# Layer 1 of a two-layer graph network: sums laid out by node, target one-hot made on ScalarE, and node blocks finished and stored inside the edge loop

## The reference, cut to what matters

```
h = relu(layernorm(x))                       # per node
z = h @ W;  el, er = <z, attn_l>, <z, attn_r>  # 8 heads of 16
e = leaky_relu(el[src] + er[dst], 0.2)
a = exp(e - segment_max(e, dst)[dst])
x = x + segment_sum(z[src] * a, dst) / segment_sum(a, dst) + bias     # layer 1

h = relu(layernorm(x))                       # per node, needs layer 1 complete
s, v = h @ W_up_s, h @ W_up_v                # the table that layer 2 gathers
w = mlp(edge_attr_8)                         # 8 -> 64 -> 64 -> 128
m = products of (s, v)[src], edge_attr_4, w  # 256 values an edge
x = x + W_out(segment_sum(m, dst) / 10)                               # layer 2
```

## Time and profile before

| | us |
|---|---|
| median of three runs | 4102.19 |
| the profiled execution | 4099.62 |
| its span | 4097.8 |
| PE busy | 3675.0 (90%) |
| PE weight load busy | 2848.9 (70%) |
| DVE busy | 1874.9 (46%) |
| ACT busy | 568.4 (14%) |
| POOL busy | 3007.4 (73%) |

### The profile page before, as it was taken

How to read it: one execution, slowest core, us unless ns; L and a number is a source line. 1 busy time by engine, 2 the same in 40 slices (tenths; PEclk the granted TensorE clock), 3 DMA queues, 4 the chain that set the end, 5 groups by cost and what they waited for, 6 DMA issues and landing times.

```text
span 4097.8 us, 68625 instructions
## 1 busy us (share of the span) xinstructions
PE 3675.0 (90%) x18070; PEld 2848.9 (70%) x18071; DVE 1874.9 (46%) x4776; ACT 568.4 (14%) x1289; POOL 3007.4 (73%) x3153
## 2 busy tenths in 40 slices
PE   2899999999999999999969889888898988899888
PEld 2677777777777777777757677666676776677666
DVE  7333333333333333333355555555555555555555
ACT  2111111111111111111131111111111111111111
POOL 3777777777777777777747777777777777777776
PEclk9555555555555555555568889898988988898998
DMA  3222222222222222222222222222222222222221
GB/s 85 56 57 57 57 57 57 57 57 57 57 57 57 57 57 57 57 57 57 57 53 59 59 60 59 60 59 60 59 59 60 59 60 59 60 60 59 59 60 51
DMA packets 259082, 239.78 MB, mean 59 GB/s; under 512 B 179890, under 2 KB 205596, under 8 KB 259068
## 3 DMA queue, kind: packets, MB, share of 16 engines
q0 software_dynamic: 100352, 212.14, 19.1%
...
q10 hardware_dynamic: 144, 0.80, 0.1%
...
...
## 4 chain that ended last, share of the span: by engine, by line
POOL 68%; issue 24%; DVE 3%; DMA 2%; PE 1%; POOLq 1%; DVEq 1%; ACT 0%; SPq 0%; ACTq 0%
POOL rows L406 68%; DMA rows<-up_tab,idx 1%; PE pair L942 1%; DVE share L895 1%; DVE dst_rel L570 0%; DVE share L885 0%; POOLq L220 0%; POOLq L434 0%; POOLq L221 0%; DVE share L770 0%; DVE share L627 0%; DVE share L898 0%; DVEq L226 0%; DMA win_dram<-share 0%; PE pair L937 0%
## 5 line engine op out<-in xcount | busy, mean ns | idle before, releaser
L406 POOL DMA_INDIRECT rows<-z_tab,idx x1568 | 1487.8, 949 | 544.2 <-issue 544.2
L406 POOL DMA_INDIRECT rows<-up_tab,idx x1568 | 1479.4, 944 | 510.8 <-issue 505.6
L1012 PE MATMUL pair<-share 128*128 128x48 f32 x3136 | 1008.0, 421 | 0.0
L1012 PEld LDWEIGHTS pair<-share 128*128 128x128 f32 x3136 | 802.9, 317 | 191.7 <-issue 184.4
L1093 PEld LDWEIGHTS pair<-share 128*128 128x128 f32 x3136 | 585.8, 219 | 454.8 <-DVE share L898 285.9
L1095 PE MATMUL pair<-share 128*128 128x144 f32 x3136 | 846.6, 359 | 0.0
L1093 PE MATMUL pair<-share 128*128 128x48 f32 x3136 | 576.9, 269 | 156.5 <-DVE share L898 154.3
L895 DVE TENSOR_TENSOR share<-rows,pair 128x384 f32<-128x384 f32 x784 | 396.9, 548 | 437.7 <-DMA rows<-up_tab,idx 409.1
L1095 PEld LDWEIGHTS pair<-share 128*128 128x128 f32 x3136 | 552.6, 220 | 0.0
L1014 PE MATMUL pair<-share 128*8 128x48 f32 x3136 | 516.2, 265 | 0.0
L806 DVE TENSOR_TENSOR share<-rows,pair 128x64 f32<-128x64 f32 x196 | 43.4, 221 | 855.0 <-DMA rows<-z_tab,idx 763.0
...
## 6 DMA issues: line engine op xcount, KB each, us to landing
rows<-z_tab,idx POOLq DMA_INDIRECT x1568
rows<-up_tab,idx POOLq DMA_INDIRECT x1568
...
ef_sb<-in_edge_f SPq DMA_DIRECT2D x198, 32.0 KB
...
y_sb<-in_edge_y SPq DMA_DIRECT2D x198, 16.0 KB
...
```

The lines of the kernel that those rows point to most:

```text
L406: pool.indirect_dma_start(out=rows[:, s, t, 0:width], out_offset=None, in_=table, in_offset=bass.IndirectOffsetOnAxis(ap=indices[:, t:t + ...
L1012: t.matmul(bank[2 + h][:, 0:WIN], msg[:, h, i, :], hot[:, s, i, :], start=(i == 0), stop=(i == T - 1), skip_group_check=True)
```

## The change

- Sums of layer 1 are formed node-major: the one-hot (now edge by 128 lanes) is the stationary operand and the messages the moving one, with exp(score) itself as a 17th column of each head, so the denominators come out of the same product. A sum goes into one of 98 half-block slots (`slot_i`), 136 wide. Rows of z_tab have 144 numbers, with ones in the 17th columns.
- The turned one-hot is no longer turned by TensorE. SyncE broadcasts the group's 1024 targets to all partitions (`load_targets`, from `dst_tab`, a float copy of the targets written to DRAM at the start), and ScalarE makes relu(1 - 2 (dst - node)^2) of it in two passes (`turned_hot`).
- The scores take three operations. `er` stays in SBUF (`er_slots`) and TensorE reads it from there by slot.
- A complete block is divided, normalized, turned, projected with `w_up`, and stored into up_tab in the loop (`finish_block`, `norm_block`, `map_up`, `store_up`). The middle stage for all blocks is gone; what is left there is the last blocks.
- Accumulators of layer 2 are cleared by VectorE and ScalarE behind the loop. All of `src` is loaded once; ScalarE copies a group's indices out of it (`set_idx`), in both layers, in place of a DMA a group.
- The set-up gets the operations that the slots need (`set_windows`), the float copy of the targets, and other memsets.

```diff
+RW = PER_HEAD + 1
+MW = HEADS * RW
+ZW = MW + HEADS
+LW = ZW + HEADS
...
+            def load_targets(s, group):
+                sp.dma_start(dst_bc[:, s % 2, :], dst_tab[bass.ds(group * GE, GE)].partition_broadcast(P)).then_inc(s_l1["in"][s % 2], 16)
+
+            def store_up(b):
+                sp.wait_ge(s_mid["row"], b + 1)
+                sp.dma_start(up_tab[bass.ds(b * P, P), :],
+                             sums_even[:, bass.ds(b, 1), 0, 0:HIDDEN].rearrange("p a f -> p (a f)"))\
+                  .then_inc(s_mid["stored"], 16)
...
+                    for s in range(U):
+                        hold(sp, s_l1["turned"], m + (s + AHEAD + 1))
+                        load_targets(s, q * U + (s + AHEAD))
+                        if s == 2:
+                            blocks(sp, q + 1, store_up)
+
+            last_blocks(sp, store_up)
...
-            pool.memset(er_win[:], 0.0).then_inc(zeroed, 1)
-            pool.memset(acc_b[:], 0.0).then_inc(zeroed, 1)
-            pool.memset(acc_a[:], 0.0).then_inc(zeroed, 1)
...
+            pool.memset(slot_i[:], 0).then_inc(zeroed, 1)
+            pool.memset(sums_all, 0.0).then_inc(zeroed, 1)
+            pool.memset(er_slots, 0.0).then_inc(zeroed, 1)
+            pool.memset(minus_id, 0.0).then_inc(zeroed, 1)
...
-                if s_l is s_l2:
-                    pool.wait_ge(s_mid["agg_staged"], NB)
-                    pool.memset(den_acc, 0.0).then_inc(zeroed, 1)
-                    pool.memset(max_acc, 0.0).then_inc(zeroed, 1)
-                    pool.memset(acc_a[:], 0.0).then_inc(zeroed, 1)
-                    table_stored(s_mid)
...
+            gather_edges(s_l1, s_l1["msg"], z_tab, ZW, passes1, 0)
+            pool.wait_ge(s_mid["stored"], 16 * NB)
+            gather_edges(s_l2, s_l2["prod"], up_tab, HIDDEN, passes, passes1 * GI)
...
+            def set_idx(s, group):
+                nc.scalar.activation(idx[:, s, :], idx_all[:, bass.ds(group, 1), :].rearrange("p a t -> p (a t)"),
+                                     ACT.Copy).then_inc(idx_set, 1)
+
+            def turned_hot(s, group, arrived):
+
+                act.wait_ge(s_l1["in"][s % 2], arrived)
+                to = hotT[:, s % 2, :]
+                nc.scalar.activation(to, dst_bc[:, s % 2, :], ACT.Square, bias=minus_id[:, bass.ds(group, 1)])\
+                    .then_inc(s_l1["square"], 1)
+                act.wait_ge(s_l1["square"], squares(group))
+                nc.scalar.activation(to, to, ACT.Relu, bias=ones[:, 0:1], scale=-2.0).then_inc(s_l1["turned"], 1)
+
+            def norm_block(b):
+
+                act.wait_ge(s_mid["mean"], b + 1)
+                nc.scalar.activation(hc_sb, x_sb[:, bass.ds(b, 1), :].rearrange("p a f -> p (a f)"), ACT.Relu,
+                                     bias=nmr1).then_inc(s_mid["centred"], 1)
+                nc.scalar.activation(std1, mv1[:, 1:2], ACT.Sqrt, bias=flags[:, 7:8]).then_inc(s_mid["norm"], 1)
+                act.wait_ge(s_mid["turned"], b + 1)
+                nc.scalar.activation(hcT_sb, bank[0][:, 0:P], ACT.Copy).then_inc(s_mid["turned_sb"], 1)
...
+            last_blocks(act, norm_block)
+            act.wait_ge(s_mid["stored"], 16 * NB)
+            nc.scalar.activation(acc[:, COLS:AUX], flags[:, 7:8].broadcast_to([P, AUX - COLS]), ACT.Copy, scale=0.0)\
+                .then_inc(G["cleared"], 1)
...
+
+                def floor_of(out, at, scale, shift):
+                    own.after(v.tensor_scalar(out, at, scale, shift, ALU.mult, ALU.add))
+                    own.after(v.tensor_scalar(out, out, ROUND, -ROUND, ALU.add, ALU.add))
+
+                floor_of(slot_f[:, :], win_f[:, :], 1.0 / HALF, -(HALF - 1) / (2.0 * HALF))
+                own.after(v.tensor_copy(slot_i[0:1, 1:NG + 1], slot_f[0:1, :]))
+                floor_of(odd_f[:, :], slot_f[:, :], 0.5, -0.25)
+                own.after(v.scalar_tensor_tensor(out=odd_f[:, :], in0=odd_f[:, :], scalar=-2.0, in1=slot_f[:, :],
+                                                 op0=ALU.mult, op1=ALU.add))
+                own.after(v.tensor_scalar(slot_f[:, :], slot_f[:, :], float(HALF), None, ALU.mult))
+
+                own.after(v.scalar_tensor_tensor(out=minus_id[:, 0:NG], in0=odd_f[:, :], scalar=col2[:, 1:2],
+                                                 in1=slot_f[:, :], op0=ALU.mult, op1=ALU.subtract))
+                own.after(v.tensor_scalar(minus_id[:, 0:NG], minus_id[:, 0:NG], col2[:, 0:1], None, ALU.subtract))
+                own.after(v.scalar_tensor_tensor(out=slot_f[:, :], in0=odd_f[:, :], scalar=-float(HALF),
+                                                 in1=slot_f[:, :], op0=ALU.mult, op1=ALU.add))
+                own.after(v.tensor_scalar(odd_f[:, :], odd_f[:, :], float(P), None, ALU.mult))
+                cols = dst_col[:, 0:NG, :]
+                own.after(v.tensor_tensor(cols, dst_rel[:, :, :], bc(slot_f[:, :], 2, T), ALU.subtract))
+                turn_back = tab_sb[:, 0:BU + 4, :].rearrange("p a f -> p (a f)")[:, 0:NG * T]\
+                    .rearrange("p (g t) -> p g t", t=T)
+                own.after(v.scalar_tensor_tensor(out=turn_back, in0=cols, scalar=float(P), in1=bc(odd_f[:, :], 2, T),
+                                                 op0=ALU.is_ge, op1=ALU.mult))
+                own.after(v.tensor_tensor(cols, cols, turn_back, ALU.subtract))
...
             def one_hot(s, group):
-
                 v.tensor_tensor(hot[:, s, :, :],
-                                bc(dst_rel[:, bass.ds(group, 1), :].rearrange("p a t -> p (a t)"), 2, WIN),
-                                bc(iota_l1, 1, T), ALU.is_equal).then_inc(s_l1["hot"], 1)
+                                bc(dst_col[:, bass.ds(group, 1), :].rearrange("p a t -> p (a t)"), 2, P),
+                                bc(iota_l1, 1, T), ALU.is_equal)
...
+            def finish_block(b):
+
+                own_block.base, own_block.n = b * 9, 0
+                even = sums_even[:, bass.ds(b, 1), 0, :].rearrange("p a f -> p (a f)")
+                odd = sums_even[:, bass.ds(b, 1), 1, :].rearrange("p a f -> p (a f)")
+                before = sums_odd[:, bass.ds(b, 1), 0, :].rearrange("p a f -> p (a f)")
+                own_block.mark(v.tensor_tensor(even[HALF:P], even[HALF:P], odd[HALF:P], ALU.add))
+                own_block.after(v.tensor_tensor(even[0:HALF], even[0:HALF], before[0:HALF], ALU.add), hold)
+                cells = even.rearrange("p (h f) -> p h f", f=RW)
+                own_block.after(v.tensor_scalar(rden, cells[:, :, PER_HEAD], TINY, None, ALU.max), hold)
                 own_block.after(v.reciprocal(rden, rden))
...
+                        own_l1.mark(v.tensor_tensor(e_sb[:, h, :, 0, :], el_e, er_e[:, :, 0, :], ALU.add))
+                        own_l1.after(v.scalar_tensor_tensor(out=e_sb[:, h, :, 1, :], in0=el_e, scalar=NEG_SLOPE,
+                                                            in1=er_e[:, :, 1, :], op0=ALU.mult, op1=ALU.add))
+                        v.tensor_tensor(e2_sb[:, h, :, :], e_sb[:, h, :, 0, :], e_sb[:, h, :, 1, :], ALU.max)\
+                            .then_inc(s_l1["score"], 1)
...
+            last_blocks(dve, finish_block)
+            v.memset(acc[:, 0:COLS], 0.0)
+            own.after(v.memset(acc[:, AUX:4 * COLS], 0.0))
...
+            def targets_er(s, group, count):
+
+                h = s % 2
+                at = pe.value_load(slot_i[0:1, bass.ds(group + 1, 1)], min_val=0, max_val=SLOTS1 - 1)
+                pe.wait_ge(s_l1["turned"], count + (AHEAD + 1))
+                for i in range(T):
+                    mm = t.matmul(bank[6 + h][:, i * 16:i * 16 + 16], hotT[:, h, i * P:(i + 1) * P],
+                                  er_flat[:, bass.ds(at, 1), :].rearrange("p a f -> p (a f)"), start=True, stop=True)
+                mm.then_inc(s_l1["er"], 1)
+
+            def map_up(b):
+
+                pe.wait_ge(s_mid["centred"], b + 1)
+                t.transpose(bank[0][:, 0:P], hc_sb, ident[:, :]).then_inc(s_mid["turned"], 1)
+                pe.wait_ge(s_mid["turned_sb"], b + 1)
+                pe.wait_ge(s_mid["row"], b)
+                t.matmul(bank[1][:, 0:P], hcT_sb, w_up[:, :], start=True, stop=True).then_inc(s_mid["lin"], 1)
...
+                                pe.wait_ge(s_l1["msg"], n * (2 * U) + (2 * U + 2 * s + i // HT + 1))
+                            if i == 0:
+                                pe.wait_ge(s_l1["added"], n * U + (s + 1))
+                            mm = t.matmul(bank[2 + h][:, 0:MW], hot[:, s, i, :], msg[:, h, i, :],
+                                          start=(i == 0), stop=(i == T - 1))
+                        mm.then_inc(s_l1["agg"], 1)
```

502 lines of the change are left out of this document (249 added, 253 removed).

## The result

The changed kernel took 4075.45 us (median of 4 runs, 4074.48 to 4084.7), the kernel before 4102.38 (4 runs, 4101.39 to 4104.24). The ratio is 0.994, with a 95% interval of 0.9928 to 0.9952, so the change gains 0.6%. Forecast: 4076, range 4060 to 4094, faster with a chance of 0.84.

The account below looks back on a forecast made before the run. GpSimd's indirect gathers and the gaps between them were taken as the bound. Set-up 96.4, layer 1 1965.4, between 34.3, layer 2 1957.0 and end 18.4 gave 4071.5, -26.3 against the span; from the 4102.19 median, 4076 us, range 4060 to 4094.

Parts of the forecast that it names:

- The set-up: Stage before the first gather: smaller memsets save time, added operations cost more; +5.2 us, first gather at 96.4.
- The cast: VectorE's first cast in the set-up: waits for GpSimd's large memsets, so ends earlier when they shrink, near 18 us.
- The DMAs that bring the windows follow VectorE: In the set-up: window transfers start after VectorE's work, with the 1.39 us wait kept; -5.4 up to 52.36.
- The operations behind: VectorE in the set-up after the windows: flags +0.4, eleven operations +3.3, three of 1568 +5.5, small memset +0.2 us.
- node_rows with the rest up to the gather: End of the set-up: products wider by 8 columns, +0.7 us, and one more GpSimd register read, +0.5.
- The loop: Layer 1: every engine's work stays hidden under the gathers' 9.98 us a group, so it stays at 1965.4 us.
- rival A: TensorE in layer 1: weight loads don't overlap in the new sums, 11.3 us a group, about 4330 us; chance 0.07.
- The middle: Last gather of layer 1 to first of layer 2: 34.3 us in place of 65.8, two blocks of 6.4 included.
- Rival C: Start of layer 2: VectorE's memsets hold GpSimd's gathers, +4 to +8, 4082 us; chance 0.14 shared with the late-start rival.
- Rival B: Layer 2 starts too late after hidden layers and clearing; up to +10, 4086 us; chance 0.14 shared with the memset rival.
- D: Gathers slow down under broadcast traffic or 576-byte rows; at 0.02 us each, 4107 us; chance 0.04.
- E: Blocks aren't finished in layer 1's loop, so the middle stays near 66 us; total 4108 us; chance 0.03.

Follow-up runs that it names:

- table: Changed kernel with the Sqrt table loaded while ScalarE waits for a block's mean; 5471.94 us on a slow chip, where the unedited changed kernel took 5488.5.
- psum: Changed kernel with bias and block ends copied into PSUM, so VectorE reads one SBUF input; 5482.52 us on a slow chip, unedited changed kernel 5488.5.

## Why the prediction was right

- *What bounds it.* On the ordinary chips GpSimd's gathers bound both layers before and after. TensorE's busy share fell by 28 points of the loop, and layer 1 didn't move beyond the execution's own pitch.
- *The set-up*: +5.2 predicted, +7.1 measured. The cast was freed, and 1.9 us sooner than summed (it ends at 16.15, forecast near 18), since the two memsets counted at 1.08 each took 0.25. All the same the windows came later than said, 48.22 for 52.36 - 5.4 = 46.96: VectorE was done at 31.47, but SyncE still had weight transfers to issue and reached the windows' stores at 34.31. "The DMAs that bring the windows follow VectorE" was the step that failed, by 1.3 us net. SyncE was late because its first seven issues, the loads of x, took 14.28 us instead of 10.14. The change adds two loads beside them on ScalarE's queue (`idx_all`, 800 KB, and the float copy's source, 792 KB), which the sum doesn't have; that these are what lengthened them wasn't tested. The operations behind cost +9.65, predicted +9.4, and node_rows with the rest up to the gather +1.6, predicted +1.2.
- *The loop*: right. The sums of 136 columns come 0.23 us apart (3.72 / 16), predicted 0.242; the passes of ScalarE take 1.13 and 1.15. Against the earlier trace rows, the rival A (4330) is out: weight loads of full rows overlap in the new sums too, 3.59 us of loads beside 3.72 of sums. TensorE is idle for 33% of the loop and not for 20%: the 16 er instructions take 2.95 us on average and not 3.84, as the granted clock is 0.61 and not the 0.50 that the sum took (1.95 us at 1.00, 3.59 at 0.50, between 1505 and 1519 us). It changes nothing in the time.
- *The middle*: 34.3 predicted, 35.2 measured, but three terms were off and nearly cancel, which is luck. With T at 2070.55, the last sums ended at T + 8.9 instead of T + 11.3 (-2.4), since the er product ran in 2.01 us at a granted clock of 0.94, and not in 3.84 at the lower one; TensorE had stood idle for 2.22 us before it. Blocks took 8.3 instead of 6.4 (+3.7 for the two): the sum has one table load of 1.28, though the paragraph on the loop counts two a block, and the trace shows both on the chain; table confirms it. And from the last row to the gather it took 3.3, not 4.75 (-1.5), for a store of 64 KB instead of 448. The rest of the chain was 0.9 longer than summed.
- *Rival C* (VectorE's clears hold the gathers) is out: L942 runs for 5.39 us from 2101.14 while the gathers from 2103.15 on take 0.95. *Rival B*: the first product comes at 2126.53, 23.4 after the first gather (24 to 28 said), and no gather of layer 2 has more than 0.3 us of idle time before it. *D*: with 0.41 of the DMA engines busy, gathers of layer 1 are as long as those of layer 2, but for the held ones. *E*: two blocks are left, as said.
- *What I missed*: that a second operation, L836 (2.60 us, two SBUF inputs), holds a gather for 3.16 us. One was held for 3.15 us in the kernel before as well, so nothing came of it.
- *The number*: 4076 predicted, 4075.45 measured, is closer than the stages are. They give 23.5 us of gain in the profiles where the forecast has 26.3, and on chip C the medians of before and of the changed kernel with its loop written out are 22.8 apart. The last 3 us of the agreement are luck, well inside the 8 us by which a pitch of 2.4 ns more moves an execution.

The page "SBUF — State Buffer" of the Trainium skill, section "Who interferes with whom", was given in the prediction for VectorE with at most one SBUF input not contending with GpSimd; psum shows it with the same operation in both forms, 6.56 us against 0.94. The page "TensorE: Matmul & The Clock Gate" of the Trainium skill, section "What overlaps and what doesn't", says that a weight load overlaps running matmuls only where the row group differs; the trace has full rows throughout, and new sums 0.23 us apart where rival A, which came out of such a rule, had 0.45.
